# Adapter rows asked for at other places, the last token half made ahead of two evictions, and GpSimd's sums held for it, at the two short tiles of a two-layer block

## The reference

```python
x = x + x @ w_eff.T                       # w_eff: quantised(weight + lora_delta) * scale + lora_delta
...
gate = lora_add(x @ W_gate.T, x, A_gate, B_gate)     # W_gate, W_up: 2752 x 1024
up   = lora_add(x @ W_up.T,   x, A_up,   B_up)
act  = silu(gate) * up
down = lora_add(act @ W_down.T, act, A_down, B_down)
x = x + down
# lora_add(base, inp, A, B) = base + (inp @ A[idx].T) @ B[idx].T * 0.5, rank 16, idx for each sequence
```

## Time and profile before

| engine | busy us | share of the span |
|---|---|---|
| TensorE, matmuls | 1573.2 | 98% |
| VectorE | 1240.1 | 77% |
| ScalarE | 566.3 | 35% |
| GpSimd | 538.7 | 34% |

### The profile page before, as it was taken

The page is one execution under the profiler, slowest core; times in us unless marked ns, Lnnn a source line. Parts: engine busy times, 40 slices in busy tenths (PEclk is TensorE's granted clock), DMA queues, the critical chain, the costliest instruction groups (busy, mean ns, idle before and its releaser), DMA issues.

```text
span 1604.2 us, 21109 instructions
## 1 busy us (share of the span) xinstructions
PE 1573.2 (98%) x6968; PEld 1294.7 (81%) x6968; DVE 1240.1 (77%) x1575; ACT 566.3 (35%) x1006; POOL 538.7 (34%) x401
## 2 busy tenths in 40 slices
PE   7999998999999999998999999999999999999999
PEld 5888886788888888886888888888888888888887
DVE  7998968788878999999867787887676576785443
ACT  6411135433333333354433333333343233233231
POOL 4410013465654555644344555555310000000000
PEclk9999999999999999999999999999999999999999
DMA  9552173677878888883335666654277677686463
GB/s 291 132 112 79 48 234 91 178 202 223 229 205 196 229 231 224 237 296 93 105 120 133 181 175 177 186 175 150 81 217 212 159 179 193 153 223 206 151 188 119
DMA packets 368460, 281.25 MB, mean 175 GB/s; under 512 B 225120, under 2 KB 266848, under 8 KB 368224
## 3 DMA queue, kind: packets, MB, share of 16 engines
q1 hardware_dynamic: 246976, 240.77, 51.6%
q10 hardware_dynamic: 119296, 33.33, 8.9%
q0 software_dynamic: 2080, 5.80, 1.8%
HBM read 166.27 MB, written 110.85 MB: 173 GB/s over the span
## 4 chain that ended last, share of the span: by engine, by line
PE 79%; DVE 1%; issue 1%; DVEq 0%
PE bank L1827 21%; PE bankA L1827 14%; PE bankC L1827 14%; PE bank L2063 10%; PE bankC L2063 7%; PE bankA L2063 6%; PE bankT L2063 3%; PE bankT L1878 1%; PE bankT L1879 1%; PE bankC L1843 1%; PE bank L1843 1%; PE bankA L1843 1%; DVE opl L1491 0%; DVE ev L1438 0%; DVE opl L1497 0%
## 5 line engine op out<-in xcount | busy, mean ns | idle before, releaser
L985 ACT CAST rh<-wt 128x512 fp32r<-128x512 f32 x253 | 155.0, 620 | 371.3 <-PE bank L1827 76.6
L1328 DVE TENSOR_TENSOR rl<-wt,rh 128x512 fp32r<-128x512 f32 x253 | 237.0, 944 | 40.2 <-ACT rh L985 40.1
L1497 DVE TENSOR_TENSOR opl<-opl,oph 128x512 fp32r<-128x512 f32 (+1 forms) x154 | 107.7, 701 | 155.6 <-ACT oph L1122 155.3
L1827 PE MATMUL bank<-xh,rh 128*128 128x512 f32 x528 | 205.7, 390 | 2.2 <-issue 2.2
L1827 PE MATMUL bank<-xl,rh 128*128 128x512 f32 x528 | 205.6, 389 | 0.0
L1827 PE MATMUL bank<-xh,rl 128*128 128x512 f32 x528 | 205.5, 389 | 0.0
L1122 ACT CAST oph<-opl 128x512 fp32r<-128x512 f32 (+1 forms) x154 | 95.5, 621 | 268.9 <-DMA opl<-LT_d 260.8
L1827 PE MATMUL bankC<-xh,rh 128*128 128x512 f32 x352 | 139.3, 396 | 7.1 <-DVE xl L1337 3.9
L1827 PE MATMUL bankC<-xl,rh 128*128 128x512 f32 x352 | 138.9, 395 | 0.0
L1827 PE MATMUL bankC<-xh,rl 128*128 128x512 f32 x352 | 138.8, 394 | 0.0
L1827 PE MATMUL bankA<-xh,rl 128*128 128x512 f32 x352 | 137.7, 391 | 0.0
(11 more groups left out here) (209 smaller groups left out, 3670.0 us busy)
## 6 DMA issues: line engine op xcount, KB each, us to landing
opl<-LT_d SPq DMA_DIRECT2D x148, 256.0 KB, 2.9
WT_d<-wt SPq DMA_DIRECT2D x88, 256.0 KB, 3.1
RT_d<-dt SPq DMA_DIRECT2D x70, 256.0 KB, 3.3
opl<-RT_d SPq DMA_DIRECT2D x70, 256.0 KB, 3.8
LT_d<-ev ACTq DMA_DIRECT2D x60, 256.0 KB, 2.6
wb<-WT_d SPq DMA_DIRECT2D x44, 256.0 KB, 3.5
wt<-WT_d SPq DMA_DIRECT2D x44, 256.0 KB, 3.5
dn<-in_L_cond_W_down_dram SPq DMA_DIRECT2D x86, 128.0 KB, 3.9
```

The costliest lines, as they stand in the source:

```text
L985: nc.scalar.copy(rh[:, v % RING, 0:KH * rows], wsrc(mm, RSRC[p])).then_inc(s_hi, 1)
L1328: dv.tensor_tensor(rl[:, v % RING, 0:KH * rows], wsrc(mm, RSRC[p]), rh[:, v % RING, 0:KH * rows].bitcast(f32), ALU.subtract).then_inc(s_lo, 1)
L1497: dv.tensor_tensor(opl[0:rows, L_AT[n % NL], :], opl[0:rows, L_AT[n % NL], :].bitcast(f32), oph[0:rows, L_AT[n % NL], :].bitcast(f32), ALU ...
L1827: last = te.matmul(OUT[p], a[:, u % RING, cols], b[:, OPND[p], k, :], start=k == 0 and n == 0, stop=k == KH - 1 and n == 2 and (p in (0, 1 ...
```

## The change

Nothing is added to or taken from the arithmetic. Three things move, at tiles 0 and 11 and the tile behind each.

Adapter rows, on ScalarE: `load_bn(1)` and `load_an(0)` stood ahead of step 0. `load_bn(1)` now stands at (0, 2) and `load_an(0)` at (0, 3) of tile 0. `load_bn(12)` and `load_an(11)` stood at (0, 5) of tile 11 and now stand at its (0, 2) and (0, 3). `load_bn(2)` and `load_bn(13)` go from (1, 6) to (1, 1) of tiles 0 and 11. `load_an(1)` and `load_an(12)` go from (1, 6) of tiles 0 and 11 to (0, 3) of tiles 1 and 12.

The last token operand, on VectorE: `lo(6)` and `x_lo(0, 6)`, which stood at step 3 behind `take(0, 2)`, now stand at step 2 ahead of it; likewise `lo(160)` and `x_lo(1, 6)` go from step 157 to step 156.

GpSimd: at steps 2 and 156 it waits for that last `x_lo` before `w_s12` of the next matrix.

```diff
--- before.py
+++ after.py
@@ -951,6 +951,8 @@
                         act_sum(it - 1, 0)
                         act_sum(it - 1, 1)
                     if p == 2 and 0 <= mm + 1 < NM:
+                        if mm in (0, NH):
+                            gp.wait_ge(s_xlo, 14 + mm // NH * 14)
                         w_s12(mm + 1)
                     if 7 * m + p == turn[2] and after:
                         act_sum(it - 1, 2)
@@ -1222,8 +1224,6 @@
                 x_hi(0, 2)
                 out_x1(TURN[KD - 1, 3])
                 x_hi(0, 3)
-                load_bn(1)
-                load_an(0)
 
                 for u in range(END):
                     mm, p, it, m = split(u)
@@ -1253,13 +1253,10 @@
                         for t in range(2):
                             ins = nc.scalar.copy(ad[:, :, t, t, 0, :], ar[:, :, t, :])
                         ins.then_inc(s_adh, 1)
-                    if (m, p) == (1, 6) and it != NJ - 1 and it + 2 < NIT:
+                    if (m, p) == ((1, 1) if first(it) else (1, 6)) and it != NJ - 1 and it + 2 < NIT:
                         load_bn(it + 2)
-                    if (m, p) == (1, 6) and it != NJ - 1 and it + 1 < NIT:
+                    if (m, p) == (1, 6) and it != NJ - 1 and not first(it) and it + 1 < NIT:
                         load_an(it + 1)
-                    if (it, m, p) == (NJ, 0, 5):
-                        load_bn(NJ + 1)
-                        load_an(NJ)
                     if live and p == 0:
                         act.wait_ge(s_pd, u + 1)
                         wait(act, s_ev, 4 * (mm - 1) + 1)
@@ -1279,6 +1276,10 @@
                             silu(it, 2)
                     if live and m == 1 and p in (3, 5) and not first(it):
                         store_raw(it, p // 2 - 1)
+                    if it < NIT and first(it) and (m, p) == (0, 2):
+                        load_bn(it + 1)
+                    if (m, p) == (0, 3) and it < NIT and it % NJ in (0, 1):
+                        load_an(it)
                     for x_ in SPLIT.get(u, ()):
                         if x_[0] == "l":
                             l_hi(int(x_[1:]))
@@ -1698,7 +1699,7 @@
                 for u in range(END):
                     mm, p, it, m = split(u)
                     r = slice(0, rows_of(jof(it)))
-                    if RING <= u + RING - 2 < 7 * NM:
+                    if RING <= u + RING - 2 < 7 * NM and u % END not in (3, 3 + END // 2):
                         lo(u + RING - 2)
                     for n in range(4):
                         v = u + 7 - n
@@ -1712,10 +1713,13 @@
                         ad_lo(it)
                     if 0 <= mm < NM and first(it) and p in (4, 6):
                         ts_lo(it // NJ, m, p // 6)
-                    if u <= 3:
+                    if u <= 2:
                         x_lo(0, u + 3)
-                    if 7 * (NM // 2) - 3 <= u < 7 * (NM // 2) + 4:
+                    if 7 * (NM // 2) - 3 <= u < 7 * (NM // 2) + 3:
                         x_lo(1, u - 7 * (NM // 2) + 3)
+                    if u in (2, 2 + END // 2):
+                        lo(u + RING - 1)
+                        x_lo(it // NJ, 6)
                     if m == 1 and p == 5 and 0 <= it < NIT and not first(it):
                         a_lo(4 * it)
                     if 0 <= it - 1 < NIT and first(it - 1) and (m, p) == (0, 4):
```

## The result

The changed kernel takes **1598.12 us** (median; 1596.05 to 1599.49), and 0.9952 of the kernel before, with an interval of 0.9941 to 0.9963. That is 8.2 us less than the 1606.32 us of the kernel before, run beside it, where 10.3 us were forecast: a gain of 0.5%, small but clear of 1 by its interval. The profiled execution took 1598.97 us, of which 1597.3 us are its span.

A forecast was written before the change was run, and what follows sets the result against it. TensorE, busy 98%, bounds the kernel; its waits stem from ScalarE's issues, VectorE's order and GpSimd's sums. First half 8.9 plus second half 1.4 gives 10.3 us off 1605.49: 1595.2 us, range 1589 to 1602.5.

The forecast's parts named there:

- First short tile: Gaps at steps 4 to 6 go; riding product of step 8 comes 5.3 us earlier, 3.6 us net of slow clock.
- Step 20: At the adapter product, the 3.60 us wait and its 2.7 us slow clock go: 6.3 us.
- I take back 1 us: Deduction of 1 us for what comes late between steps 20 and 26, where adapter splits have little to spare.
- Second short tile: Steps 158 to 160 on time, riding product of step 162 2.4 us earlier after a 6 us wait; net 1.4 us.
- Edit 1's new places at no cost: ScalarE's moved adapter-row issues, with high parts late behind them, priced at 0; bounds 0 to 4.2 us per half.
- (a): Rival: time won at the short tile is given back at step 20; 1601 us, chance 0.20.
- (b): Rival: the wait only moves to the riding products; about 1604 us, chance 0.10.
- (c): Rival: ScalarE becomes the bound through eight issues at (0, 3) in four tiles; 1609.5 us, chance 0.05.
- (d): Rival: no slow clock behind the new waits and sums cost VectorE nothing; 1588 us, chance 0.04.
- forecast's own range: 1589 to 1599 us, from bounds on late high parts (0 to 4.2 us) and delay beside sums (0 to 6.6).
- ScalarE's queue: Cited skill section gives ScalarE a strict first-in first-out queue of 8, so nothing behind eight issues passes them.

The follow-up runs named there:

- token_hold: The changed kernel with ScalarE's adapter-row issues back at their old places: 1606.1 us, ratio 1.0 to the kernel before.
- rows_hold: The changed kernel with the last token half back behind the two evictions, GpSimd's wait kept: 1601.7 us, ratio 0.9971 to the kernel before.
- Edit 1: ScalarE's adapter-row issues moved; run alone against the kernel before: 1598.2 us, ratio 0.9947.
- no_hold: The changed kernel without GpSimd's wait for the last token half: 1604.2 us, ratio 0.9979 to the kernel before.
- an_late: The changed kernel with the eight `an` issues of tiles 0 and 11 at (0, 6) instead of (0, 3): 1599.3 us in one execution.
- acts_an_late: acts_late with the eight `an` issues of tiles 0 and 11 at (0, 6) instead of (0, 3): 1593.2 us, ratio 0.9921 to the kernel before.
- acts_late: The changed kernel with GpSimd's third weight sum behind the first ts_lo and the activation's sums behind both: 1594.5 us, ratio 0.9932 to the kernel before.
- edit 2: Last token half made ahead of two evictions on VectorE; added to the kernel before together with Edit 1 only: 1604.2 us, ratio 0.9979.
- edit 3: GpSimd's sums held until the last token half; added to the kernel before together with Edit 1 only: 1601.7 us, ratio 0.9971.
- hold_ts: The changed kernel with one more GpSimd wait, at steps 4 and 158, until both ts_lo are made: 1599.4 us, ratio 0.9955 to the kernel before.

## Why the prediction was right, and where it was not

The direction, the places and most sizes held; the time came 2.9 us above the forecast (1598.1 against 1595.2), inside the range of 1589 to 1602.5. Of the 2.9 us, 0.8 are the kernel before, which took 1606.32 us beside this result and 1605.49 when the forecast was made; 2.1 are missing from the gain. By the steps:

- **First short tile, right.** The three waits went, the riding product came 5.3 us earlier (lead at step 8), as forecast, with a wait of 2.12 us (forecast 2.3) and a slow clock of 3.4 us behind it. Net 3.7 us at step 10; forecast 3.6. That the clock fell was partly luck: behind waits of 2.33 us (token_hold) and 3.56 us (rows_hold) at this product it did not, and without its cost of 1.6 us this tile would have given 5.3. VectorE paid (1.10 - 0.68) + (1.80 - 0.88) = 1.3 us beside the sums, as forecast.
- **Step 20, 5.3 us where 6.3 were forecast.** The idle 3.73 us of the earlier trace rows are gone. The corresponding split starts at 285.00 with no wait, which is 7.8 us earlier counted from step 0 (forecast 7.7). But VectorE's chain from it to the adapter split took 1.3 us longer than before (15.5 against 14.2): the first two parts of the gated product took 2.62 us beside GpSimd's sums where they had taken 1.32, and 0.5 us of idle time came ahead of them. That left 0.80 us of wait. The clock was 1.00 in its place, as forecast:

```profile
300.00:307.00 7.00, 6.34 (x28) 5.29 (x29) 5.72 (x8) 3.62 (x7) 1.68 (x1) 1.00 1.13 297
```

- **"I take back 1 us", too little.** 0.7 us went between steps 22 and 28 (at 326.20 TensorE waits 0.39 us for an adapter split), 0.2 by step 31, and 0.7 at step 115 (a wait of 0.45 us at 586.84, for which I have no cause): 1.8 in all. So the first half gave 7.2 us; forecast 8.9.
- **Second short tile: the term that was mis-sized.** It was forecast at 1.4 us and gave 0.4 between steps 154 and 168. I put the saving at 6.3 us and what VectorE pays beside the held sums at 4.0. Three of the saved terms were there, 4.4 us: all x_lo pairs at 2.35 us, and the split between them at 0.68. The fourth, 1.9 us at 737.91, was not: I took that delay for the work of the five sums, but GpSimd's next three caused it, and they stand at the same ts_lo in after. They cost 1.95 us before and 2.6 now, as they reach the split ahead of it too. The five held sums cost 2.7 us, less than my 4.0. In all 6.3 us of delay became 5.3. So the riding product came 0.8 us earlier counted from step 154, not 2.4. The wait of 6 us ahead of it was forecast and came (2.40 + 3.52), and so did the clock's fall. That cost some 2.1 us (half of the 4.25 us that TensorE is busy in it) where before had lost 1.7, and 0.8 less 0.4 is the gain of 0.4:

```profile
731.20:738.00 6.80, 4.25 (x10) 3.41 (x11) 6.74 (x9) 1.93 (x4) 4.65 (x4) 0.50 0.32 94
```

- **Edit 1's new places at no cost, right.** Steps 22 and 176 don't wait. The silu of tile 0 starts at 282.17, where ts_hi ended at 280.22; one conversion and a table load of 1.28 us stand between them. In no_hold the issues at (0, 3) do cost something (1.63 us of VectorE), so the price of nothing holds for the order of after.
- **Rivals.** (a) fell with step 20: 5.3 of 6.3 us stayed. (b) holds for the second short tile, 6.03 us of waits against 6.17, and not for the first. (c) fell: an_late and acts_an_late show under 0.4 us for the issues at (0, 3). (d) did not come: both riding products have a slow clock behind their waits, and the sums cost 5.3 us in the second tile.
- **The range.** Its lower end, 1589, is 1595.2 less 4.0 and 1.3 us (sums at no cost in either tile) and less the 1.0 taken back. The upper end of the forecast's own range, 1599, takes in one of its two bounds; both, 2.6 and 4.2 us, give 1602. The result lies inside either.
- **ScalarE's queue.** The order and depth of ScalarE's queue stand in the Trainium skill, "TensorE: Matmul & The Clock Gate", but under the section "Architectural detail: the array is 16× 32×32, not 1× 128×128", and not under the one that the prediction names. The traces agree that nothing passes eight issues: in acts_late the conversions behind them wait 2.05 us (shown below).

What the prediction did not see is how the edits hang together. It gave edit 2 and edit 3 a price each and added them. The runs show that on top of edit 1, edit 2 alone takes 5.7 us from the lead (8.7 to 2.9), edit 3 alone 1.8, and both 0.8, which is within chance. Without edit 1 both together give 2.1 (token_hold).

## What to carry to other kernels

When an engine is held back so that its work does not disturb another, name the delayed instructions and look up which work stands beside each of them. Here one of four delays belonged to three other sums, which the hold left where they were. Then follow the engine's whole queue, and what the moved work makes late. Put such sums beside evictions from PSUM or beside work with slack; holding them until the critical instruction is made, in the order in which others need them, won 6.3 us of lead over the plain hold here, up to 1.6 of them by the clock. And after each removal of a wait ask what is late next: twice here (hold_ts, acts_an_late) it was the next adapter product, some 10 us on, and it took back what had been won.

## What the runs showed of the hardware that was not expected

- For VectorE's instructions with two SBUF inputs beside GpSimd's sums, the price did not depend on their size. A pair of ts_lo of 0.88 us takes 2.83, a pair of x_lo of 2.35 us takes 4.51: 2.0 and 2.2 us more, about 1 us for each instruction. A single split of 0.68 us takes 1.78. So small critical instructions are the worst place for a sum.
- ScalarE's DMA issues, some 0.46 us each, held only what was handed over behind them. In acts_late the four parts of ts_hi ran beside the eight issues of `an`, and the two conversions behind the issues waited 2.05 us:

```profile
718.15 0.90 ACT L1067 ACTIVATE ts<-ev,half_of 32x256 fp32r<-32x256 f32 x2
718.64 2.36 ACTq L1040 DMA_DIRECT2D an<-Ad_d  x5
721.10 1.14 ACT L991 CAST rh<-wt 128x512 fp32r<-128x512 f32 x2 [2.05 <-issue]
```

- The length of a wait alone does not tell whether a slow clock follows. Waits of 2.33 us (token_hold) and 3.56 us (rows_hold) at the first tile's riding product have a granted clock of 1.00 behind them, one of 2.12 us (after) has 0.50. Two short waits can have it too. In acts_late waits of 0.77 and 0.86 us, 1.8 us apart, have a granted clock of 0.50 behind them for 3.4 us; in acts_an_late waits of 0.52 and 0.86 us at the same place have 1.00. That step is worth 1.5 us (lead at step 163).
